# One more ScalarE pass in place of a VectorE operation for the clip of 1 - a² in a recurrent stage

## What is computed

```python
x_conv = cb + sum((xp[:, k:k + Lx, :] * cw[:, k] for k in range(KCONV)))
r_t = sigmoid(x_conv @ wrw.T + wrb)
i_t = sigmoid(x_conv @ wiw.T + wib)
a_t = sigmoid(la) ** (8.0 * r_t)
b_t = sqrt(clip(1.0 - a_t * a_t, 1e-06, None)) * (i_t * x_conv)
h = _parallel_scan(a_t, b_t)
return _rmsnorm(h @ wow.T, nw)
```

## Time and profile before

| what | us |
|---|---|
| median of 3 runs | 2050.89 (2049.95 to 2053.34) |
| the profiled execution | 2053.53 |
| its span | 2051.8 |
| the recurrent stage in it | up to about 397 |
| busy in the span: TensorE, VectorE, ScalarE, GpSimd | 1673.2, 1201.0, 1083.9, 613.3 |

### The profile page before, as it was taken

The page is one execution under the profiler, slowest core; times in us unless marked ns, Lnnn a source line. Parts: engine busy times, 40 slices in busy tenths (PEclk is TensorE's granted clock), DMA queues, the critical chain, the costliest instruction groups (busy, mean ns, idle before and its releaser), DMA issues. The chain is left out here.

```text
span 2051.8 us, 33423 instructions
## 1 busy us (share of the span) xinstructions
PE 1673.2 (82%) x9958; PEld 1130.4 (55%) x9959; DVE 1201.0 (59%) x1940; ACT 1083.9 (53%) x2285; POOL 613.3 (30%) x562
## 2 busy tenths in 40 slices
PE   4988888562399879899999999932699999999990
PEld 1333333261299746444444444421599999999990
DVE  6999998486611154358999999268432332333224
ACT  6777776540033234137888888613355555555554
POOL 0000000000156322211222222100376767767760
PEclk9899999765599979989999999875799999999995
DMA  4000000124022096603333333075244444444417
GB/s 169 1 0 0 0 0 0 44 83 164 19 66 65 22 314 252 108 10 78 75 97 95 95 95 90 22 266 191 79 66 73 69 70 69 68 68 68 69 21 246
DMA packets 146024, 173.68 MB, mean 85 GB/s; under 512 B 29427, under 2 KB 110718, under 8 KB 145792
## 3 DMA queue, kind: packets, MB, share of 16 engines
q1 hardware_dynamic: 104160, 128.29, 20.5%
q0 software_dynamic: 33536, 43.71, 12.1%
q10 hardware_dynamic: 8224, 0.39, 0.2%
HBM read 111.77 MB, written 66.45 MB: 87 GB/s over the span
## 5 line engine op out<-in xcount | busy, mean ns | idle before, releaser
L1283 PEld LDWEIGHTS f_ht_ps<-f_XT,f_WS 128*128 128x128 f32 x2944 | 358.5, 193 | 15.8 <-DVE f_WS L1376 2.7
L1283 PE MATMUL f_ht_ps<-f_XT,f_WS 128*128 128x128 f32 x2944 | 361.7, 276 | 3.5 <-ACT f_XT L1324 3.5
L1291 PE MATMUL f_y_ps<-W,f_HT 128*128 x1472 | 347.9, 379 | 0.0
L2103 DVE TENSOR_REDUCE att_MX<-att_s_ps 128x2 f32<-128x1024 f32 x256 | 305.6, 1216 | 65.4 <-PE att_s_ps L1859 65.0
L1249 POOL DMA_INDIRECT moe<-f_Y,TOK x184 | 277.8, 1510 | 184.1 <-ACT f_Y L1349 156.3
L2066 ACT ACTIVATE att_PT<-att_st_ps 128x512 f32<-128x512 f32 x512 | 278.5, 595 | 74.7 <-PE att_st_ps L1884 66.7
L1291 PEld LDWEIGHTS f_y_ps<-W,f_HT 128*128 128x128 f32 x1472 | 265.5, 190 | 28.6
L1240 POOL DMA_INDIRECT XG<-x,TOK x184 | 193.8, 1053 | 232.2 <-issue 149.6
L1376 DVE COPY f_WS<-W 128x1024 f32 x184 | 131.6, 715 | 209.4 <-PE f_ht_ps L1283 128.7
L297 PE MATMUL rec_gate<-rec_XC,rec_W 128*128 128x512 f32 x384 | 189.6, 647 | 68.5 <-ACT rec_R L199 42.8
L1884 PE MATMUL att_st_ps<-att_Q,att_K 50*128 50x512 f32 x512 | 221.5, 488 | 19.6 <-ACT att_PT L2066 19.2
(11 more groups left out here) (265 smaller groups left out, 2230.3 us busy)
## 6 DMA issues: line engine op xcount, KB each, us to landing
W<-in_w SPq DMA_DIRECT2D x48, 512.0 KB, 9.8
att_Q<-qk_pairs SPq DMA_DIRECT2D x192, 64.0 KB, 2.8
att_K<-qk_pairs SPq DMA_DIRECT2D x192, 64.0 KB, 2.9
qk_pairs<-prj_HI SPq DMA_DIRECT2D x16, 512.0 KB, 3.8
qk_pairs<-prj_LO SPq DMA_DIRECT2D x16, 512.0 KB, 5.1
hidden<-in_xT SPq DMA_DIRECT2D x8, 512.0 KB, 7.9
x<-n_Y SPq DMA_DIRECT2D x8, 512.0 KB, 3.0
prj_X<-x SPq DMA_DIRECT2D x8, 512.0 KB, 8.7
```

Of the source, the lines that this page charges most:

```text
L1283: mm = nc.tensor.matmul(ht_ps[r % 2][:, f * P:(f + 1) * P], WS[r % 2][:, at:at + P], XT[r % 2][:, c], start=(c == 0), stop=(c == DC - 1))
L1291: mm = nc.tensor.matmul(y_ps[r % 2][:], HT[r % 2][:, f], W2[:, bass.ds(e * W_EXPERT + f * D, D)], start=(f == 0), stop=(f == FC - 1))
L2103: nc.vector.tensor_reduce(MX[n % 2][:, qc, :, p], s_ps[m % 2][:], AX.X, ALU.max).then_inc(s_mx, 1)
```

## The change

`decay_square` is removed from VectorE, with its semaphore `v_ready`. In its place the root on ScalarE gets a first pass: Relu of (1 - 1e-6) - A2, in place, with scale -1 and the bias read from the first column of a new small tile `least`. The Ln that follows has scale 1 now and adds 1e-6 from the second column of that tile. ScalarE's wait for VectorE's operation becomes one for its own squares of the decay. Two memsets on GpSimd fill the tile, and the waits for the constants count to 7 in place of 5.

```diff
--- before.py
+++ after.py
@@ -101,6 +101,7 @@
         floor = st.sb("floor", [P, S])
         mean_w = st.sb("mean_w", [P, P])
         eps = st.sb("eps", [P, 1])
+        least = st.sb("least", [P, 2])
         shape = [P, DC, GB, S]
         XC = [st.sb(f"XC{k}", shape) for k in range(XCS)]
         R = st.sb("R", shape)
@@ -127,7 +128,6 @@
         s_gate_mm = st.sem("gate_product")
         s_gate = st.sem("gate_ready")
         s_a2 = st.sem("a2_ready")
-        s_v = st.sem("v_ready")
         s_la_used = st.sem("m_ready")
         s_d = st.sem("step_ready")
         s_ix = st.sem("ix_ready")
@@ -170,6 +170,8 @@
             nc.gpsimd.memset(floor[:], LOG_FLOOR).then_inc(s_const, 1)
             nc.gpsimd.memset(mean_w[:], 1.0 / D).then_inc(s_const, 1)
             nc.gpsimd.memset(eps[:], RMS_EPS).then_inc(s_const, 1)
+            nc.gpsimd.memset(least[:, 0:1], 1.0 - 1e-6).then_inc(s_const, 1)
+            nc.gpsimd.memset(least[:, 1:2], 1e-6).then_inc(s_const, 1)
 
         @block.scalar
         def _(act):
@@ -224,8 +226,9 @@
                 nc.scalar.activation(RT[u % 2][:], RT[u % 2][:], ACT.Exp).then_inc(s_ratio, 1)
 
             def root(u):
-                act.wait_ge(s_v, u + 1)
-                own.after(nc.scalar.activation(A2[u % 2][:], A2[u % 2][:], ACT.Ln, scale=-1.0))
+                act.wait_ge(s_a2, DC * (u + 1))
+                own.after(nc.scalar.activation(A2[u % 2][:], A2[u % 2][:], ACT.Relu, scale=-1.0, bias=least[:, 0:1]))
+                own.after(nc.scalar.activation(A2[u % 2][:], A2[u % 2][:], ACT.Ln, bias=least[:, 1:2]))
                 nc.scalar.activation(A2[u % 2][:], A2[u % 2][:], ACT.Exp, scale=0.5).then_inc(s_root, 1)
 
             def squares_out(u):
@@ -248,7 +251,7 @@
 
             act.wait_ge(s_cv, 16)
             conv_start(0)
-            act.wait_ge(s_const, 5)
+            act.wait_ge(s_const, 7)
             for l in range(LAYERS):
                 own.after(nc.scalar.activation(LNA[:, l, :, 3:4], CV[:, l, :, COL_LOG_A:COL_LOG_A + 1], ACT.Sigmoid))
             for l in range(LAYERS):
@@ -280,7 +283,7 @@
 
         @block.tensor
         def _(pe):
-            pe.wait_ge(s_const, 5)
+            pe.wait_ge(s_const, 7)
 
             def gate_products(u, first, last):
                 l, g = where(u)
@@ -369,10 +372,6 @@
                 dve.wait_ge(s_conv, DC * (u + 1))
                 nc.vector.tensor_tensor(IX[u % 2][:], I[:], XC[u % XCS][:], ALU.mult).then_inc(s_ix, 1)
 
-            def decay_square(u):
-                dve.wait_ge(s_a2, DC * (u + 1))
-                nc.vector.tensor_scalar(A2[u % 2][:], A2[u % 2][:], 1.0, -1e-6, ALU.subtract, ALU.min).then_inc(s_v, 1)
-
             def state(u):
                 dve.wait_ge(s_root, u + 1)
                 dve.wait_ge(s_ix, u + 1)
@@ -397,14 +396,12 @@
                                                        op0=ALU.mult, op1=ALU.mult).then_inc(s_norm, 1)
 
             dve.wait_ge(s_cv, 16)
-            dve.wait_ge(s_const, 5)
+            dve.wait_ge(s_const, 7)
             conv(0)
             conv(1)
             dve.wait_ge(s_lna, 2 * LAYERS)
             decay(0)
             for step in range(UNITS + 1):
-                if step < UNITS:
-                    decay_square(step)
                 if step + 2 < UNITS:
                     conv(step + 2)
                 if step < UNITS:
```

## The result

| | before | changed |
|---|---|---|
| median | 2052.11 us (4 runs, 2049.95 to 2053.50) | 2070.78 us (4 runs, 2070.08 to 2071.80) |
| profiled execution, its span | 2053.53, 2051.8 us | 2070.08, 2068.3 us |

The change makes the kernel slower by 18.7 us: the ratio is 1.0092, with a 95% interval of 1.0075 to 1.0110. The forecast was 22.9 us, and the time lies in the range given.

The account below looks back on a forecast made before the run. The prediction took the loop of ScalarE's unbroken part and the gate phase shared with TensorE as the bound. Added passes of 16.2 us plus 6.7 us of clock made 22.9 us, so 2073.8 us, range 2064 to 2082 us.

Parts of the forecast that it names:

- The bound: Recurrent stage: ScalarE's unbroken part and the gate phase shared with TensorE close the loop; VectorE follows a few tenths behind.
- The Relu's size: ScalarE's root: the added Relu pass with the bias operands costs 2.12 us a unit, 1.94 us at the low end.
- rival (5): Relu on ScalarE needs another table: 24 loads of 1.28 us, some 31 us more, 2105 us; chance 0.03.
- The cover: Behind ScalarE's root, 0.92 us of the new pass goes into vanishing waits for mean squares, net 1.20 us a step.
- The first and the last unit: Units 0 and 11: nothing hides the new pass, so the whole 2.12 us counts in each.
- Steps without the clock: Steps 1 to 10 of the recurrent stage: 10 x 1.20 = 12.0 us added, TensorE's clock effect left out.
- The clock: TensorE's gate-bank wait grows from 3.44 to about 4.6 us; slower products cost 6.7 us, between 0 and 11.8 us.
- the sum without the clock: Recurrent stage: ten steps plus first and last unit, 12.0 + 2.1 + 2.1 = 16.2 us; low end 14.1 us.
- (3): VectorE is the real bound, so its 1.15 us a unit comes out: 13.8 us faster, 2037 us; chance 0.04.
- (1): TensorE's clock keeps its mixture of steps: 14.1 to 16.2 us and up to 3 more, 2065 to 2070 us; chance 0.21.
- (2): TensorE's lower clock lasts a whole gate phase: 12 us or more of clock cost, about 2082 us; chance 0.09.
- (4): No change: the new pass falls into ScalarE's 6.7 idle us a step, 2051 us; chance 0.03.

Follow-up runs that it names:

- the kernels with fillers: Three extra unused matmuls in TensorE's long wait of every step, added to the changed kernel (2060.0 us) and to the kernel before (2045.9 us).

## Why the prediction was right, step by step

**The bound.** Right for the seven steps in which TensorE's clock falls: ScalarE's unbroken part and the gate phase set them, VectorE follows. The operation put back at no measurable price in the steps, and the kernel without either operation, 13.8 us being absent, show it. Wrong for the three short steps. I wrote that the loop never passes through VectorE but for a 0.77 us wait, and left that wait out of the sum. That wait was the sign of a second loop, through VectorE, 0.9 us longer than the first at the full clock (29.06 against 28.18 us). With the clock held at 1.00 it sets seven of the ten steps of the kernel before (29.07 us). I had also read VectorE's 0.54 us wait as that of the short steps; it stands in a step of 29.88 us. In a short one it is half of that, and the rest of VectorE's step runs on:

```profile
186.98 1.23 DVE L374 TENSOR_SCALAR rec_A<-rec_A 128x2048 f32<-128x2048 f32 x1 [0.26 <-ACT rec_A L219]
```

**The Relu's size.** 2.00 us, and the Ln's growth from 1.91 to 2.00 us: 2.12 us a unit, as worked out. No table load stands among the three passes; rival (5) is out.

**The cover.** 0.92 us forecast; 8.48 - 7.26 = 1.22 us net was measured against 1.20 us. The second Relu shows that nothing is left of it.

**The first and the last unit.** The last: 2.1 us forecast, 2.09 measured. The first: 2.1 forecast, 1.32 measured. The shift was there, but the sixteen products at 51.41 took 9.27 us where those at 49.00 had taken 10.08 us, 0.8 us less at the lower clock. How long those take differs from one execution to the next: the kernels with fillers have none in step 0, which is there 24.60 and 27.41 us long, 2.8 us apart. The 2.1 us lies between the two measured differences, and no one pair can size it.

**Steps without the clock.** 12.0 us forecast, 9.75 us with the clock held at 1.00 in both kernels. What was too large is 10 x 1.20: in the seven steps that close through VectorE the price is 1.07 us, 0.9 us less in all. The first of the ten was even 0.15 us shorter (30.13 against 30.28 us), since before, with fillers, VectorE had catching up to do in it (30.07 us of work); that is the other 1.35 us. Steps held back by the clock grew by the forecast amount, 31.09 - 29.88 = 1.21 us.

**The clock.** 6.7 us forecast, 4.4 us measured. That the three short steps would turn into common ones came true: none is left. That four more would become like the dearest did not: one did and passed it (32.45 us, where 30.92 + 1.20 makes 32.12), one came halfway (31.59 us), two were common ones (31.09 us), and four were a little cheaper (30.77 to 30.97 us). The direction was right and the size was a guess between bounds, as the text says. The longer wait of the kernel with two Relus shows the direction more strongly than I would have put it. The errors in this term and in the sum without the clock lie on the same side and add up: 22.9 us forecast, 18.7 us measured.

**The rivals.** (3), VectorE as the bound, has its place: with four gate banks it is true, and its point is the one named, ScalarE having time to spare. For the stage of the kernel as it is, it is refuted, 13.8 us being absent; only the three short steps were VectorE's, by 0.9 us each. (1), the clock unchanged, gave 2065 to 2070 us and came within 1 us of the measured time, nearer than the forecast, but its mechanism was not what happened: the mixture changed, and the sum without the clock was smaller. (2), the lower clock through a whole gate phase, didn't come: the dearest sixteen products took 10.19 us, in one step. (4), the pass lost in ScalarE's idle time, is refuted by the change itself and by the second Relu.

## What to carry to other kernels

An engine that is busy 98% of the time need not be the bound of every step: here VectorE's loop set the three steps at the full clock, by 0.9 us, and another loop the seven others. Look for the loop in which nobody waits for that engine, and price an edit by both loops. Work moved from the fullest engine to one with 7 us to spare in 29 cost its length less the waits that stood behind it, since the spare time lay in another part of the step, and the longer gap that it left on TensorE cost clock on top. The same edit cost nothing that could be measured once the other loop had been relieved (here by two more banks), so try the relief first.

## What the runs showed of the hardware

GpSimd needs 7.08 us for a two-operation tensor-scalar on 128 x 2048 fp32 elements with no convolution tap beside it and 7.8 us with one, about six times VectorE's 1.23 us; with four gate banks it takes 8.7 to 9.1 us in all units but the first, and no run here shows why. VectorE's taps beside it are not all slowed: one in each step takes 5.5 us in place of 1.28 us, the others what they always take.

TensorE's granted clock fell in or behind seven of ten gaps of 3.44 us, all ten of 4.65 us, and all ten of 6.59 us. The sixteen products behind them took 7.13 us at 1.00, and 8.52 to 10.19 us behind the gap of 4.65 us. Both levels appear within one step: in the kernel before the granted clock is 0.50 from 79 to 85 us, the gap having ended at 80.14, and 1.00 from 86 us on. The fall can also come once the products run again: in the changed kernel the clock is still 1.00 from 82 to 83 us, where a gap of 4.65 us ends (82.95), and 0.50 from 84 to 86 us. A longer gap doesn't always cost more: behind 6.59 us (two Relus) the sixteen products took 9.94 us, behind 6.80 us (the operation on GpSimd) 9.49 to 9.71 us. What decides how long the clock stays low is not settled by these runs.
